# A chain of four graph layers on one core: 64 of 196 source record gathers made in the first convolution, and ScalarE's second-product copy placed later in the prefill

## The chip, the cores and the metric

The program runs on one core of one Trainium2 chip. The time is the device time of one execution in microseconds (us), 3544.22 as the median of three runs (3536.5 to 3548.16). Engines: PE is TensorE, DVE VectorE, ACT ScalarE, POOL GpSimd; SP only issues plain transfers. POOL issues the gathers (indirect DMAs). A cut-off "q" (SPq) is an engine's sequencer.

## The reference, cut to what matters

50,000 nodes with 128 features, 25,000 edges sorted by destination. Four graph layers, each added to its input and layer-normalised. The change touches the work of the first one:

```python
def _gcn_conv(x, W, b, src, dst, dinv, n_nodes):
    h = x @ W
    norm = dinv[src] * dinv[dst]
    msgs = h[src] * norm[:, None]
    out = segment_sum(msgs, dst, num_segments=n_nodes)   # src, dst with a self loop for every node
    return out + b

h = relu(_gcn_conv(x, W1, b1, src, dst, dinv, N))
x = layernorm(x + _gcn_conv(h, W2, b2, src, dst, dinv, N))
x = layernorm(x + mean of 8 relations)       # 8 weights and a root
x = layernorm(x + attention over 8 relations)
x = layernorm(x + relu(sum over 16 relations))
```

## The kernel before, in words

Edges are padded to 25,088 = 49 steps of 4 tiles of 128 (`NB` = 49, `BT` = 4, `KT` = 196 tiles). Nodes are worked in 98 chunks of 4 x 128 rows (`NCH` = 98). A node without an incoming edge needs no gather: its two convolution products are dense. That is the prefill. Nodes with edges get their rows in the edge stages.

Stages run one after the other; each is a block in which every engine has its own program, ordered by semaphores, and between two stages all engines meet and POOL clears the semaphores.

**Prefill** (`prefill_stage`). Per chunk: SP loads 256 KB of x; PE turns it (L594), ACT copies it out of PSUM (`xT`, L646), PE multiplies by W1 (L634), ACT applies the relu (`hT`, L677), PE multiplies by W2 (L602), ACT copies that second product out of PSUM (`g1`, L653), DVE adds x and b2 and takes the statistics, ACT makes the standard deviation (`sd1`, L668), DVE the scale and shift, and ACT the normalised rows (`x1`, four instructions, L660). SP stores `g1` and `x1`, 256 KB each (L547). All is software-pipelined: in turn c ScalarE works on chunk c (`xT`, `hT`), c-1 (`g1`), c-2 (`sd1`) and c-3 (`x1`), and `g1` and `x1` have two buffers each, so a buffer is written only when its store of two chunks ago has landed. In the first 49 chunks DVE and PE also count each node's edges (one-hot rows, L692, L694; L610); after chunk 48 DVE makes from the counts a table with a record per node: the row that holds its result, and `dinv`. SP stores that table (`t_info`).

POOL meanwhile gathers: 196 times 128 rows of x by destination (L576, kept for all stages), and, once `t_info` has landed, 196 times 128 records of 8 bytes by source (`m_info`, L580). The stage ends when all of these have landed and all stores too.

**First convolution** (`edge_stage` with `CONV1`, 49 steps). POOL gathers 4 tiles of source rows a step (L1101) into one of two buffers; it may start on step s when ACT has read step s-2 (`scaled_ready`). ACT scales the rows by `norm_col` (L1139), and the nodes' own rows (L1144); PE sums both and turns them (L1263, L1264); DVE scans along equal destinations (L1329); PE, ACT, PE make the two products (L1249, L1165, L1276); ACT writes `c_new` (L1195) and SP stores it. The same engines work through 49 dense chunks of the next layer in the same turns (`DenseLayers`: L860, L867, L876, L885, L902). `norm_col` (all 196 tiles) and `row_int` are made from the records by two DVE instructions at the stage's start (L1295, L1296). The second convolution uses `row_int` as its gather index.

In one turn of the first convolution ScalarE's order is: `dense_sd`, `scaled`, `own`, `dense_x1T`, `hT`, `dense_x` (L885), `c_new`.

Of the kernel before, what the change touches and what calls it, by code (L numbers as in the profile page):

```python
# [16 lines left out]
BT = 4  # L17
# [3 lines left out]
KT = EP // TE  # L21
# [6 lines left out]
NA = TA // BT  # L28
FAR = 65536
PAD_DST, PAD_SRC, PAD_TYPE = 60000, 0, -1  # L30
EPS = 1e-5
SLOPE = 0.2
LOW = -1.0e30
# [7 lines left out]
def runs(b, first=0, last=NB - 1):  # L41

    return not static(b) or first <= b <= last
# [429 lines left out]
def prefill_stage(nc, io, m):  # L473


    with ExitStack() as ctx:
# [91 lines left out]
        @block.gpsimd  # L568
        def _(pool):
            pool.memset(lower[:, :], 1.0).then_inc(lower_ready, 1)  # L570
            hold(pool, lower_ready, 1)
            pool.affine_select(out=lower[:, :], in_=lower[:, :], compare_op=ALU.is_ge, fill=0.0, base=0,
                               pattern=[[1, P]], channel_multiplier=-1).then_inc(lower_ready, 1)

            for k in range(KT):
                pool.indirect_dma_start(m.xd[:, k * D:(k + 1) * D], None, io["x"],  # L576
                                        bass.IndirectOffsetOnAxis(ap=m.dst_int[:, k:k + 1], axis=0)).then_inc(gathered, 16)
            hold(pool, info_stored, 16)
            for k in range(KT):
                pool.indirect_dma_start(m.info[:, k, :], None, m.info_table,  # L580
                                        bass.IndirectOffsetOnAxis(ap=m.src_int[:, k:k + 1], axis=0)).then_inc(gathered, 16)
            hold(pool, gathered, 2 * KT * 16)

        @block.tensor
        def _(pe):
# [51 lines left out]
        @block.scalar  # L637
        def _(act):
            def body(c, slot, first_half):
                q, o = slot % 2, 1 - slot % 2  # L640
                s = c
                if runs(s, 0, END):
                    act.wait_ge(x_turned, s + 1)
                    if runs(s, 2, END):
                        act.wait_ge(xw1_done, s - 1)
                    act.activation(xT[:, q, :], T[q][:, :], ACT.Copy).then_inc(xT_copied, 1)  # L646
                s = c - 1
                if runs(s, 0, END):
                    act.wait_ge(hw2_done, s + 1)
                    if runs(s, 2, END):  # L650
                        act.wait_ge(g1_stored[o], of_slot(s - 2, o, 16))
                        act.wait_ge(z1_ready, s - 1)
                    act.activation(flat(g1[:, o]), U[o][:, :], ACT.Copy).then_inc(g1_ready, 1)  # L653
                s = c - 3
                if runs(s, 0, END):
                    act.wait_ge(scale1_ready, s + 1)
                    if runs(s, 2, END):
                        act.wait_ge(x1_stored[o], of_slot(s - 2, o, X1_STORES[o]))
                    for j in range(BT):
                        last = act.activation(x1[:, o, j, :], z1[:, o, j, :], ACT.Identity,  # L660
                                              bias=shift1[:, o, j:j + 1], scale=scale1[:, o, j:j + 1])
                    last.then_inc(x1_ready, 1)
                s = c - 2
                if runs(s, 0, END):
                    act.wait_ge(mv1_ready, s + 1)
                    if runs(s, 1, END):
                        act.wait_ge(scale1_ready, s)
                    act.activation(sd1[:, :], mv1[:, :, 1], ACT.Sqrt, bias=m.eps[:, 0:1]).then_inc(sd1_ready, 1)  # L668
                if static(c) and c == HALF:
                    act.wait_ge(degree_ready, 1)  # L670
                    act.activation(root_of[:, :], degree[:, :], ACT.Sqrt, bias=m.ones[:, 0:1]).then_inc(rooted, 1)
                s = c
                if runs(s, 0, END):
                    act.wait_ge(xw1_done, s + 1)
                    if runs(s, 2, END):
                        act.wait_ge(hw2_done, s - 1)
                    act.activation(hT[:, q, :], H[q][:, :], ACT.Relu, bias=m.b1[:, 0:1]).then_inc(hT_ready, 1)  # L677
            chunks(act, body)

        @block.vector  # L680
        def _(v):
# [121 lines left out]
            def body(c, slot, first_half):  # L803
# [7 lines left out]
            chunks(v, body)  # L811


def rows_of(table, chunk):
# [170 lines left out]
def edge_stage(nc, io, m, kind, source, out, weights=None, n_rel=0):  # L985
# [5 lines left out]
    with ExitStack() as ctx:  # L991
# [18 lines left out]
        if kind == CONV2:  # L1010
# [19 lines left out]
            sem(n) for n in ("summed", "stats_ready", "scale_ready", "biased_ready", "squared", "norm_ready",  # L1030
                             "own_ready"))
        var_ready, sd_ready, shift_ready = sem("var_ready"), sem("sd_ready"), sem("shift_ready")
        T, H, B, S = m.psum[0:2], m.psum[2:4], m.psum[4:6], m.psum[6:8]
        LAST = NB - 1
        index = {CONV1: m.src_int, ATTEND: m.slot_int}.get(kind, m.row_int)
# [55 lines left out]

        @block.gpsimd
        def _(pool):
            for b in range(-2, NB + 3):
                s = b + 2
                if runs(s, 0, LAST):
                    if runs(s, 2):
                        hold(pool, turned if factor is None else scaled_ready, s - 1)
                    for j in range(BT):
                        k = s * BT + j  # L1100
                        pool.indirect_dma_start(rows[:, s % 2, j, :], None, source,  # L1101
                                                bass.IndirectOffsetOnAxis(ap=index[:, k:k + 1], axis=0))\
                            .then_inc(gathered[s % 2], 16)
                    if recorded is not None:
                        for j in range(2):
                            k = first_recorded + s * 2 + j
                            pool.indirect_dma_start(m.order8, bass.IndirectOffsetOnAxis(ap=m.order_int[:, k:k + 1], axis=0),  # L1107
                                                    m.row_int[:, k:k + 1], None, bounds_check=P * TA - 1, oob_is_err=False)\
                                .then_inc(recorded, 16)
                s = b - lag  # L1110
                if kind == SUM and runs(s, 0, LAST):
                    hold(pool, new_ready, s + 1)
                    for j in range(BT):
                        k = s * BT + j
                        pool.indirect_dma_start(out, bass.IndirectOffsetOnAxis(ap=m.last_int[:, k:k + 1], axis=0),  # L1115
                                                new[:, s % 2, j, :], None, bounds_check=NP - 1, oob_is_err=False)\
                            .then_inc(kept[s % 2], 16)
            if recorded is not None:
                hold(pool, recorded, KT // 2 * 16)
            if kind == SUM:  # L1120
                for q in range(2):
                    hold(pool, kept[q], of_slot(LAST - (LAST - q) % 2, q, KEPT))

        @block.scalar
        def _(act):
            if kind == CONV1:
                act.wait_ge(norm_ready, 3)

            def body(b, q):
                o = 1 - q  # L1130
# [161 lines left out]
        @block.vector  # L1292
        def _(v):
            if kind == CONV1:
                v.tensor_tensor(m.norm_col[:, :], m.info[:, :, 1], m.dinv_col[:, :], ALU.mult).then_inc(norm_ready, 1)  # L1295
                v.tensor_copy(m.row_int[:, :], m.info[:, :, 0]).then_inc(norm_ready, 1)  # L1296
                v.tensor_tensor(squares[:, :], m.dinv_col[:, :], m.dinv_col[:, :], ALU.mult).then_inc(squared, 1)
                v.wait_ge(squared, 1)
                v.tensor_tensor(self_col[:, :], squares[:, :], m.ends_col[:, :], ALU.mult).then_inc(norm_ready, 1)

            def relate(s, q, relations):

# [54 lines left out]
            def normalise(s, q):  # L1357

                if kind == CONV1 or not runs(s, 0, LAST):
# [4 lines left out]
                v.scalar_tensor_tensor(out=shift[:, q, :], in0=norm[1][:, :, 0], scalar=-1.0, in1=scale[:, q, :],  # L1364
                                       op0=ALU.mult, op1=ALU.mult).then_inc(shift_ready, 1)

            def add_b2(s, q):
# [25 lines left out]
            def body(b, q):  # L1393
                o = 1 - q
                if conv:
                    if kind == CONV1:
                        add_b2(b - 4, q)
                    scan(b - 1, o)
                    if kind == CONV1:
# [345 lines left out]
def build(nc, io):  # L1745
# [13 lines left out]
    with ExitStack() as ctx:  # L1759
# [14 lines left out]
            sb(n, [P, KT], I32) for n in ("dst_int", "hi_int", "lo_int", "src_int", "last_int", "row_int"))  # L1774
        m.order_int, m.slot_int, m.tile_type = sb("order_int", [P, KT], I32), sb("slot_int", [P, KT], I32), sb("tile_type", [1, TA], I32)
        m.info = sb("info", [P, KT, 2])
        m.xd = sb("xd", [P, KT * D])
        constants_stage(nc, m)
        with nc.sbuf_tensor("m_halo", [QR, 258], I32) as m.halo, nc.sbuf_tensor("m_rows", [QR, 4, 256], I32) as m.rows:
# [39 lines left out]
```

## Time and profile before

| what | value |
|---|---|
| median of three runs | 3544.22 us (3536.5 to 3548.16) |
| the profiled execution | 3547.79 us, its span 3546.1 us |
| busy share of the span | PE 68%, DVE 68%, POOL 63%, ACT 48%, PE weight loads 43% |
| mean granted TensorE clock | 0.835 of full speed |
| prefill | 61.7 to 609 us of the span |
| first convolution | 610 to 965 us |
| source record gathers | 196, 1001 ns each, 338 to 600 us |

A share of the whole span says little here, since every stage has another limit. The trace is therefore read stage by stage: which engine idles, and for whom.

### The profile page before, as it was taken

What the parts mean: (1) busy time and instruction counts of PE and PEld (TensorE: products, weight loads), DVE (VectorE), ACT (ScalarE), POOL (GpSimd) and SP (SyncE); (2) the same over time, 40 slices, a digit from 0 to 9 for tenths busy, and PEclk for the clock granted to TensorE, in tenths of its full rate; (3) what the DMA queues carried; (4) which work ended last, traced back from release to release, by engine and by line L of the source; (5) the groups of instructions that cost most, each with busy time, mean ns of one, the idle gap of its engine ahead of it and who ended that gap; (6) DMA issues with size and microseconds to landing.
All of it is one profiled execution on the core that took longest, in us unless ns stands there. A gap on an engine that the chain in (4) does not pass through costs nothing. (4 is left out here: it accounts for less than half of the span.)

```text
span 3546.1 us, 55088 instructions
## 1 busy us (share of the span) xinstructions
PE 2412.7 (68%) x9989; PEld 1522.5 (43%) x9990; DVE 2423.7 (68%) x7395; ACT 1716.3 (48%) x4719; POOL 2219.3 (63%) x2178
## 2 busy tenths in 40 slices
PE   2775761777655665999976765453233599999997
PEld 1443440666555654344433335443222244444443
DVE  7998661788778886899961112223566588888886
ACT  1774772888745554455444445554577311111111
POOL 2777776555377774777747766552666366666664
PEclk9997885999878887999988995555555699999998
DMA  2664552555445443333327776554577411111111
GB/s 64 215 215 145 173 178 62 157 172 173 149 126 152 147 149 94 82 91 91 93 82 244 255 238 168 167 172 138 150 206 211 124 40 45 48 49 50 51 52 34
DMA packets 294009, 465.22 MB, mean 131 GB/s; under 512 B 65978, under 2 KB 120793, under 8 KB 293930
## 3 DMA queue, kind: packets, MB, share of 16 engines
q1 hardware_dynamic: 224682, 351.70, 30.9%
q0 software_dynamic: 69248, 112.70, 13.1%
q14 instruction: 59, 0.48, 0.0%
q8 instruction: 20, 0.33, 0.0%
HBM read 247.81 MB, written 220.22 MB: 132 GB/s over the span
## 5 line engine op out<-in xcount | busy, mean ns | idle before, releaser
L1221 PE MATMUL bank<-sum_masked,sum_w 128*128 128x512 f32 x1568 | 691.2, 594 | 1.4 <-DVE sum_masked L1311 1.4
L1311 DVE SCALAR_TENSOR_TENSOR sum_masked<-sum_typ,sum_col 128x512 f32<-128x512 bf16 x784 | 488.6, 683 | 19.4 <-ACT sum_col L1151 17.3
L1221 PEld LDWEIGHTS bank<-sum_masked,sum_w 128*128 128x128 f32 x1568 | 291.4, 191 | 332.3 <-issue 268.9
L1221 PE MATMUL bank<-mean_masked,mean_w 128*128 128x512 f32 x784 | 376.7, 610 | 18.9 <-DVE mean_masked L1311 18.9
L1101 POOL DMA_INDIRECT sum_rows<-t_x,m_row_int x196 | 224.3, 1144 | 239.2 <-PE bank L1267 168.6
L1151 ACT ACTIVATE sum_col<-bank 128x512 f32<-128x512 f32 x49 | 29.3, 597 | 578.9 <-PE bank L1267 565.4
L1101 POOL DMA_INDIRECT mean_rows<-t_x,m_row_int x196 | 233.7, 1192 | 101.0 <-issue 57.3
L1514 POOL DMA_INDIRECT at_us<-t_u,m_slot_int x196 | 185.2, 945 | 148.8 <-PE bank L1633 79.7
L1101 POOL DMA_INDIRECT c_rows<-x_dram,m_src_int x196 | 185.3, 945 | 147.0 <-ACT c_scaled L1139 90.7
L1101 POOL DMA_INDIRECT att_rows<-t_h,m_slot_int x196 | 185.2, 945 | 141.0 <-POOLq L94 54.8
L1115 POOL DMA_INDIRECT out_dram<-sum_new,m_last_int x196 | 218.5, 1115 | 87.5 <-issue 67.2
L1311 DVE SCALAR_TENSOR_TENSOR mean_masked<-mean_typ,mean_col 128x512 f32<-128x512 bf16 x392 | 252.6, 686 | 17.1 <-ACT mean_col L1151 17.1
L1504 POOL DMA_INDIRECT at_xs<-t_x,at_order x204 | 192.9, 945 | 100.1 <-issue 63.8
L1101 POOL DMA_INDIRECT c_rows<-t_g,m_row_int x196 | 188.7, 963 | 99.2 <-issue 55.8
L576 POOL DMA_INDIRECT m_xd<-x_dram,m_dst_int x196 | 207.7, 1060 | 64.5 <-issue 64.5
L580 POOL DMA_INDIRECT m_info<-t_info,m_src_int x196 | 196.2, 1001 | 69.3 <-issue 66.0
L1107 POOL DMA_INDIRECT order<-m_row_int,m_order_int x196 | 198.5, 1013 | 59.7 <-issue 59.7
L602 PE MATMUL bank<-m_w,pf_hT 128*128 128x128 f32 x784 | 126.0, 309 | 142.6 <-ACT pf_hT L677 142.6
L1221 PEld LDWEIGHTS bank<-mean_masked,mean_w 128*128 128x128 f32 x784 | 130.3, 190 | 196.3 <-DVE mean_masked L1311 151.0
L1525 DVE COPY at_made<-bank 128x512 f32<-128x512 f32 x51 | 35.3, 691 | 251.3 <-PE bank L1601 251.3
L1652 DVE TENSOR_TENSOR_SCAN at_dst<-at_nxt,at_dst,bank 128x512 f32<-128x512 bf16 x48 | 61.4, 1280 | 203.9 <-DMA at_nxt<-p_next 202.6
L1601 PE MATMUL bank<-at_both,at_xsT 128*128 x408 | 154.3, 475 | 64.1 <-issue 61.5
(322 smaller groups left out, 6045.7 us busy)
## 6 DMA issues: line engine op xcount, KB each, us to landing
pf_xc<-x_dram SPq DMA_DIRECT2D x98, 256.0 KB, 3.0
t_g<-pf_g SPq DMA_DIRECT2D x98, 256.0 KB
t_x<-pf_x SPq DMA_DIRECT2D x98, 256.0 KB
c_dense_x<-t_x SPq DMA_DIRECT2D x98, 256.0 KB, 3.4
t_x<-c_dense_x SPq DMA_DIRECT2D x98, 256.0 KB, 3.4
t_h<-at_made SPq DMA_DIRECT2D x51, 256.0 KB, 3.1
t_u<-at_made SPq DMA_DIRECT2D x51, 256.0 KB, 3.6
c_same<-p_same SPq DMA_DIRECT2D x98, 128.0 KB, 3.4
```

Of the source, the lines that this page charges most:

```text
L576: pool.indirect_dma_start(m.xd[:, k * D:(k + 1) * D], None, io["x"], bass.IndirectOffsetOnAxis(ap=m.dst_int[:, k:k + 1], axis=0)).then_inc ...
L580: pool.indirect_dma_start(m.info[:, k, :], None, m.info_table, bass.IndirectOffsetOnAxis(ap=m.src_int[:, k:k + 1], axis=0)).then_inc(gathe ...
L602: last = pe.matmul(U[o][:, j * D:(j + 1) * D], hT[:, o, j * D:(j + 1) * D], m.w2[:, :], start=True, stop=True)
L1101: pool.indirect_dma_start(rows[:, s % 2, j, :], None, source, bass.IndirectOffsetOnAxis(ap=index[:, k:k + 1], axis=0))\
L1107: pool.indirect_dma_start(m.order8, bass.IndirectOffsetOnAxis(ap=m.order_int[:, k:k + 1], axis=0), m.row_int[:, k:k + 1], None, bounds_che ...
L1115: pool.indirect_dma_start(out, bass.IndirectOffsetOnAxis(ap=m.last_int[:, k:k + 1], axis=0), new[:, s % 2, j, :], None, bounds_check=NP - ...
L1221: pe.matmul(H[q][:, :], w[:, r, :], masked[:, r % MASKS, :], start=(r == 0), stop=(r == n_rel - 1))\
L1311: v.scalar_tensor_tensor(out=masked[:, r % MASKS, :], in0=typ[:, q, :], scalar=float(r), in1=col[:, q, :], op0=ALU.is_equal, op1=ALU.mult) ...
L1504: pool.indirect_dma_start(xs[:, s % 2, j, :], None, m.tables["X2"], bass.IndirectOffsetOnAxis(ap=order[:, k:k + 1], axis=0))\
L1514: pool.indirect_dma_start(us[:, s % 2, j, :], None, m.tables["U"], bass.IndirectOffsetOnAxis(ap=m.slot_int[:, k:k + 1], axis=0))\
L1601: last = pe.matmul(M[q][j // 2][:, (j % 2) * 2 * D:(j % 2 + 1) * 2 * D], xsT[:, q, j * TE:(j + 1) * TE], both[:, bass.ds(r * (2 * D), 2 * D)],
L1652: v.tensor_tensor_scan(dst[:, q, ::-1], nxt[:, q, ::-1], TD[q][:, ::-1], start, ALU.mult, ALU.add)\
```

## The change

64 of the 196 source record gathers (`INFO_LATE`) are no longer made in the prefill. In the first convolution POOL issues four of them behind the rows of every second step, 0 to 30. `norm_col` is made per step on DVE (49 instructions on 128x4 in place of one on 128x196), each waiting for the records by count, and ScalarE's `scaled` waits for it. `row_int` is made at the start of the second convolution, and POOL waits for it there. In the prefill ScalarE's copy `g1` stands behind `x1` instead of ahead of it.

```diff
@@ prefill, POOL
-            for k in range(KT):
-                pool.indirect_dma_start(m.info[:, k, :], None, m.info_table, ...).then_inc(gathered, 16)
-            hold(pool, gathered, 2 * KT * 16)
+            for k in range(KT - INFO_LATE):
+                gather_info(pool, m, k)
+            hold(pool, gathered, KT * 16)
+            hold(pool, m.info_gathered, (KT - INFO_LATE) * 16)
@@ prefill, ScalarE, in body(c, slot, first_half)
                     act.activation(xT[:, q, :], T[q][:, :], ACT.Copy).then_inc(xT_copied, 1)
-                s = c - 1
-                    ...
-                    act.activation(flat(g1[:, o]), U[o][:, :], ACT.Copy).then_inc(g1_ready, 1)
                 s = c - 3
                     ...
                     last.then_inc(x1_ready, 1)
+                s = c - 1
+                    ...
+                    act.activation(flat(g1[:, o]), U[o][:, :], ACT.Copy).then_inc(g1_ready, 1)
                 s = c - 2
@@ edge_stage, POOL
+            if kind == CONV2:
+                hold(pool, rows_known, 1)
@@
+                    if kind == CONV1 and s % 2 == 0 and s // 2 < INFO_LATE // BT:
+                        for j in range(BT):
+                            gather_info(pool, m, KT - INFO_LATE + s // 2 * BT + j)
@@ edge_stage, ScalarE
+                    if kind == CONV1:
+                        act.wait_ge(norm_ready, s + 1)
@@ edge_stage, DVE
-                v.tensor_tensor(m.norm_col[:, :], m.info[:, :, 1], m.dinv_col[:, :], ALU.mult).then_inc(norm_ready, 1)
-                v.tensor_copy(m.row_int[:, :], m.info[:, :, 0]).then_inc(norm_ready, 1)
+            if kind == CONV2:
+                v.tensor_copy(m.row_int[:, :], m.info[:, :, 0]).then_inc(rows_known, 1)
@@
+            def norms(s):
+                v.wait_ge(m.info_gathered, (s + 1) * BT * 16)
+                v.tensor_tensor(at(m.norm_col, s), m.info[:, bass.ds(s * BT, BT), 1], at(m.dinv_col, s), ALU.mult)\
+                    .then_inc(norm_ready, 1)
```

POOL's order from the prefill into the first convolution, before (`m_xd` are the destination rows, `m_info` the source records, `c_rows` the source rows; the branches and the ISA row are the meeting of the engines and the clearing of semaphores):

```order
L576 DMA m_xd<-x_dram,m_dst_int 128x128 x196
L580 DMA m_info<-t_info,m_src_int 128x2 x196
L476 UNCONDITIONAL_BRANCH
L95 UNCONDITIONAL_BRANCH
L98 ISA x36
L94 UNCONDITIONAL_BRANCH
L1092 UNCONDITIONAL_BRANCH
L1101 DMA c_rows<-x_dram,m_src_int 128x128 x196
```

And with the change, POOL at the same place, down to step 6:

```order
L577 DMA m_xd<-x_dram,m_dst_int 128x128 x196
L817 DMA m_info<-t_info,m_src_int 128x2 x132
L477 UNCONDITIONAL_BRANCH
L96 UNCONDITIONAL_BRANCH
L99 ISA x36
L95 UNCONDITIONAL_BRANCH
L1100 UNCONDITIONAL_BRANCH
L1111 DMA c_rows<-x_dram,m_src_int 128x128 x4
L817 DMA m_info<-t_info,m_src_int 128x2 x4
L1111 DMA c_rows<-x_dram,m_src_int 128x128 x8
L817 DMA m_info<-t_info,m_src_int 128x2 x4
L1111 DMA c_rows<-x_dram,m_src_int 128x128 x8
```

64 gathers have left the row ahead of the meeting, and stand in fours among the rows of the first 32 steps: 12 gathers where there were 8 in every two steps. Behind them the remaining rows follow as before.

ScalarE's order in a turn of the prefill, before (`pf_g` is the copy `g1`, `pf_x` the rows `x1`):

```order
L646 ACTIVATE pf_xT<-bank 128x512
L653 ACTIVATE pf_g<-bank 128x512
L660 ACTIVATE pf_x<-pf_z,pf_shift,pf_scale 128x128 x4
L668 ACTIVATE pf_sd<-pf_mv,m_eps 128x4
L677 ACTIVATE pf_hT<-bank,m_b 128x512
```

And ScalarE's order in the same turn with the change:

```order
L647 ACTIVATE pf_xT<-bank 128x512
L654 ACTIVATE pf_x<-pf_z,pf_shift,pf_scale 128x128 x4
L663 ACTIVATE pf_g<-bank 128x512
L669 ACTIVATE pf_sd<-pf_mv,m_eps 128x4
L678 ACTIVATE pf_hT<-bank,m_b 128x512
```

The copy has moved past four instructions; each of the two keeps the waits that it had (the copy for PE's second product, the rows for their scale and for the landing of a store).

## Rows read from the trace of the kernel before

**Rows 1.** Busy time by stretch: PE, PEld, DVE, ACT, POOL (count), clock, DMA share, GB/s.

```profile
62.00:295.00 233.00, 164.95 (x889) 111.14 (x890) 216.77 (x971) 168.14 (x385) 176.13 (x172) 0.96 0.66 211
332.00:536.00 204.00, 142.55 (x630) 94.18 (x630) 132.17 (x540) 151.23 (x358) 149.54 (x148) 0.82 0.57 177
640.00:945.00 305.00, 228.46 (x1700) 192.52 (x1699) 249.00 (x941) 275.32 (x849) 162.55 (x173) 1.00 0.55 171
```

**Rows 2.** Timeline of POOL: start, duration, instruction, idle time before it and releaser.

```profile
599.23 0.94 POOL L580 DMA_INDIRECT m_info<-t_info,m_src_int  x1 [0.30 <-issue]
610.15 0.99 POOL L1101 DMA_INDIRECT c_rows<-x_dram,m_src_int  x1 [9.97 <-POOLq L94]
```

**Rows 3.** The dense work's end: SP's last store, and busy time by stretch.

```profile
555.13 0.33 SPq L547 DMA_DIRECT2D t_x<-pf_x  x1
...
556.00:557.00 1.00, 0.00 (x0) 0.00 (x0) 0.00 (x0) 0.00 (x0) 0.69 (x2) 0.50 0.72 257
```

**Rows 4.** Timeline of the first convolution's end: DVE's last instruction, POOL's next.

```profile
963.35 1.14 DVE L1382 SCALAR_TENSOR_TENSOR m_xd<-c_new,m_dinv_col,c_biased 128x128 f32<-128x128 f32 x4
968.92 0.94 POOL L1101 DMA_INDIRECT c_rows<-t_g,m_row_int  x1 [36.45 <-POOLq L94]
```

**Rows 5.** ScalarE's groups from 332 to 536 us: busy, mean ns, idle before.

```profile
L653 ACT ACTIVATE pf_g<-bank 128x512 f32<-128x512 f32 x45 | 26.9, 597 | 50.7 <-PE bank L602 42.6 <-DVE pf_z L797 8.1
```

**Rows 6.** Timelines of ACT, DVE and SP, one turn of the prefill's second half.

```profile
442.09 1.65 ACT L660 ACTIVATE pf_x<-pf_z,pf_shift,pf_scale 128x128 f32<-128x128 f32 x4
443.65 0.28 ACT L668 ACTIVATE pf_sd<-pf_mv,m_eps 128x4 f32<-128x4 f32 x1
...
443.96 0.18 DVE L779 RECIPROCAL pf_scale<-pf_sd 128x4 f32<-128x4 f32 x1 [1.03 <-ACT pf_sd L668]
...
444.98 0.69 DVE L797 TENSOR_TENSOR pf_z<-pf_g,pf_xb 128x512 f32<-128x512 f32 x1
...
447.00 0.33 SPq L547 DMA_DIRECT2D t_x<-pf_x  x1
```

**Rows 7.** How long a store takes to land: SP and ACT timelines, DMA issues (KB each, median us).

```profile
233.20 0.33 SPq L547 DMA_DIRECT2D t_x<-pf_x  x1
...
236.75 1.64 ACT L660 ACTIVATE pf_x<-pf_z,pf_shift,pf_scale 128x128 f32<-128x128 f32 x4 [0.56 <-DMA t_x<-pf_x]
...
t_x<-c_dense_x SPq DMA_DIRECT2D x98, 256.0 KB, 3.4
...
t_x<-m_xd SPq DMA_DIRECT2D x49, 256.0 KB, 4.3
```

**Rows 8.** Timeline of PE, a turn at the lower clock.

```profile
444.55 2.08 PE L602 MATMUL bank<-m_w,pf_hT 128*128 128x128 f32 x8 [0.55 <-ACT pf_hT L677]
446.42 1.91 PE L634 MATMUL bank<-pf_xT,m_w 128*128 128x512 f32 x2
```

**Rows 9.** Timelines of POOL, PE and ACT, a step of the first convolution.

```profile
749.97 0.94 POOL L1101 DMA_INDIRECT c_rows<-x_dram,m_src_int  x1 [2.14 <-ACT c_scaled L1139]
...
751.01 0.46 PE L1263 MATMUL bank<-m_ident,c_scaled 128*128 128x128 f32 x2 [1.73 <-ACT c_own L1144]
...
754.15 1.14 ACT L1195 ACTIVATE c_new<-bank,m_dinv_col 128x128 f32<-128x128 f32 x4 [0.69 <-PE bank L1276]
```

**Rows 10.** Timeline of ACT: `scaled` of steps 0, 31 and 32.

```profile
616.78 1.27 ACT L1139 ACTIVATE c_scaled<-c_rows,m_norm_col 128x128 f32<-128x128 f32 x4 [61.67 <-DMA c_rows<-x_dram,m_src_int]
...
823.65 1.28 ACT L1139 ACTIVATE c_scaled<-c_rows,m_norm_col 128x128 f32<-128x128 f32 x4
830.48 1.28 ACT L1139 ACTIVATE c_scaled<-c_rows,m_norm_col 128x128 f32<-128x128 f32 x4
```

**Rows 11.** POOL's groups: 337.9 to 560 us, 560 to 601, 640 to 931.

```profile
L580 POOL DMA_INDIRECT m_info<-t_info,m_src_int x164 | 166.0, 1012 | 59.6 <-issue 56.2 <-DMA t_info<-pf_info_rows 3.4
...
L580 POOL DMA_INDIRECT m_info<-t_info,m_src_int x33 | 31.2, 944 | 10.1 <-issue 10.1
...
L1101 POOL DMA_INDIRECT c_rows<-x_dram,m_src_int x172 | 162.5, 945 | 129.9 <-ACT c_scaled L1139 90.3 <-issue 39.7
```

More of the change, by code:

```diff
@@ L30 @@
 PAD_DST, PAD_SRC, PAD_TYPE = 60000, 0, -1
+INFO_LATE = 64
 EPS = 1e-5
@@ L646, in body @@
                     act.activation(xT[:, q, :], T[q][:, :], ACT.Copy).then_inc(xT_copied, 1)
-                s = c - 1
[L648 to L652, printed above, removed]
-                    act.activation(flat(g1[:, o]), U[o][:, :], ACT.Copy).then_inc(g1_ready, 1)
                 s = c - 3
@@ L662, in body @@
                     last.then_inc(x1_ready, 1)
+                s = c - 1
+                if runs(s, 0, END):
+                    act.wait_ge(hw2_done, s + 1)
+                    if runs(s, 2, END):
+                        act.wait_ge(g1_stored[o], of_slot(s - 2, o, 16))
+                        act.wait_ge(z1_ready, s - 1)
+                    act.activation(flat(g1[:, o]), U[o][:, :], ACT.Copy).then_inc(g1_ready, 1)
                 s = c - 2
@@ L811, in _, with gather_info @@
             chunks(v, body)
+def gather_info(pool, m, k):
+    pool.indirect_dma_start(m.info[:, k, :], None, m.info_table,
+                            bass.IndirectOffsetOnAxis(ap=m.src_int[:, k:k + 1], axis=0)).then_inc(m.info_gathered, 16)
 def rows_of(table, chunk):
@@ L1032, in edge_stage @@
         var_ready, sd_ready, shift_ready = sem("var_ready"), sem("sd_ready"), sem("shift_ready")
+        self_ready, rows_known = sem("self_ready"), sem("rows_known")
         T, H, B, S = m.psum[0:2], m.psum[2:4], m.psum[4:6], m.psum[6:8]
@@ L1126, in _ @@
             if kind == CONV1:
-                act.wait_ge(norm_ready, 3)
+                act.wait_ge(self_ready, 1)
             def body(b, q):
@@ L1294, in _ @@
             if kind == CONV1:
-                v.tensor_tensor(m.norm_col[:, :], m.info[:, :, 1], m.dinv_col[:, :], ALU.mult).then_inc(norm_ready, 1)
-                v.tensor_copy(m.row_int[:, :], m.info[:, :, 0]).then_inc(norm_ready, 1)
                 v.tensor_tensor(squares[:, :], m.dinv_col[:, :], m.dinv_col[:, :], ALU.mult).then_inc(squared, 1)
                 v.wait_ge(squared, 1)
-                v.tensor_tensor(self_col[:, :], squares[:, :], m.ends_col[:, :], ALU.mult).then_inc(norm_ready, 1)
+                v.tensor_tensor(self_col[:, :], squares[:, :], m.ends_col[:, :], ALU.mult).then_inc(self_ready, 1)
+            if kind == CONV2:
+                v.tensor_copy(m.row_int[:, :], m.info[:, :, 0]).then_inc(rows_known, 1)
             def relate(s, q, relations):
@@ L1365, in normalise @@
                                        op0=ALU.mult, op1=ALU.mult).then_inc(shift_ready, 1)
+            def norms(s):
+                if not runs(s, 0, LAST):
+                    return
+                v.wait_ge(m.info_gathered, (s + 1) * BT * 16)
+                v.tensor_tensor(at(m.norm_col, s), m.info[:, bass.ds(s * BT, BT), 1], at(m.dinv_col, s), ALU.mult)\
+                    .then_inc(norm_ready, 1)
             def add_b2(s, q):
@@ L1396, in body @@
                     if kind == CONV1:
+                        norms(b + 2)
                         add_b2(b - 4, q)
@@ L1776, in build @@
         m.info = sb("info", [P, KT, 2])
+        m.info_gathered = nc.alloc_semaphore("info_gathered")
         m.xd = sb("xd", [P, KT * D])
```

2 lines of the change are left out of this document (removed).

## The prediction

> **What bounds the kernel now.** Stages follow one another, so I read the trace by stretches first: busy time of each engine in each [rows 1]. The reader is to see three regimes. In the prefill's first half VectorE is busy 216.77 of 233 us and bounds it. In the second half no engine is: ScalarE, the busiest, has 151.23 of 204 us, so a ring of waits bounds it. In the first convolution ScalarE has 275.32 of 305 us and bounds it.
>
> Next the ends of the two stages, in the timelines. POOL's last record gather of the prefill starts at 599.23 and the first convolution's first gather at 610.15 [rows 2]. The dense work was done long before: SP's last store goes out at 555.13, and its transfer is the one stretch with busy DMA, 556 to 557 [rows 3]. So from 557 to 602 the kernel waits for POOL alone, and POOL's row of gathers is what ends the prefill.
>
> Then the idle time inside the two rings, from the groups and timelines. In the prefill ScalarE stands 50.7 us, in 45 turns, ahead of the copy of the second product, 42.6 of it for PE [rows 5]. In the first convolution POOL waits 2.14 us a step for ScalarE to free a buffer [rows 9], 90.3 us from 640 to 931 [rows 11]. These are the two covers on which the change draws.
>
> **The change part by part.** The sum is made against the profiled execution, 3547.79 us (span 3546.1), which is 3.6 us above the median of the runs shown, 3544.22.
>
> *1. 64 gathers leave the prefill.* Beside the dense work a record gather takes 1.012 us and 0.34 between two: (166.0 + 56.2)/164 = 1.355 [rows 11]. POOL begins them at 338; 132 end at 338 + 132 x 1.355 = 517. Then the dense work is last, at 557. From the end of everything to POOL's next gather there are two rows to go by: the first convolution's end, where VectorE stops at 964.5 and POOL starts at 968.92, 4.4 us [rows 4], and the prefill's own, where the last gather leaves POOL at 600.2 and the next starts 10 us later [rows 2], some 8 of them after it can have landed. I take the first, since here too POOL will have stopped earlier: 557.2 + 4.4 = 562 in place of 610: 48 us less. By the other it is 44.
>
> *2. The copy behind the normalised rows.* A turn takes 204/45 = 4.53 us [rows 1, 5]. The wait ahead of the copy goes, since four instructions (442.09 to 443.65, 1.56 us [rows 6]) now stand in it. What is late next? The rows come 1 us or so earlier in the turn, and they wait for the store of two turns ago. That ring, from [rows 6]: rows 1.56, copy 0.60 [rows 5], deviation to VectorE's start 0.31, to the end of the sum `pf_z` 1.71 (443.96 to 445.67), to SP's store 1.33 (447.00), landing 3.4 (the median of stores of this size in the first convolution, under about the same 170 GB/s [rows 1, 7]), together 8.91 for two turns: 4.46 a turn. Before, the copy was not in this ring: 8.31, 4.16 a turn, hidden. The other limit is PE at its lower clock (1.2 GHz): 1.87 from the second product to the next first one and 1.91 for that one [rows 8], and the relu's copy and the handovers, some 0.75: 4.53. The granted clock is 0.82 in this half [rows 1], so 1.2 GHz in about 36% of the time. 0.64 x 4.46 + 0.36 x 4.53 = 4.49: 0.04 x 49 turns = 2 us less. In the first half VectorE's 233/49 = 4.75 a turn stays above 4.46: nothing. Ends: the whole wait gone would give 50.7/45 x 49 = 55 us, but POOL's own end, 517 + 10 = 527, cuts that to 35; a landing of 3.55, as in the first half [rows 7], gives 4.53, nothing; one of 4.3, the slowest median in the trace [rows 7], gives 4.9, and 18 us more. I take 2, by the row nearest in load.
>
> *3. The 64 gathers in the first convolution.* POOL's four gathers a step take 0.945 each and 0.30 between two, 1.245 [rows 11]; a record gather takes the same when nothing runs beside it, 0.944 and 0.31 [rows 11]. In two steps POOL has now 12: 14.94 us. Two steps of ScalarE take 13.67 (830.48 - 823.65 = 6.83 [rows 10]). So the cover does not do: POOL becomes the bound of the first 32 steps. 16 x 14.94 = 239, and 1.65 until ScalarE starts on the landed rows (610.15 + 4 x 1.245 to 616.78): the scaling of step 31 starts 240.7 after the first gather. Before it was 823.65 - 610.15 = 213.5. Afterwards ScalarE goes on at 6.83 a step as before: 27 us more. Ends: 0, if ScalarE's waits took all of it; 16 x 12 x 1.355 + 1.65 - 213.5 = 48, if gathers are as slow as in the prefill. I take 27, since the 172 rows of this very stage all but agree on 945 ns.
>
> The Trainium skill, on the page SBUF — State Buffer (section Who interferes with whom), holds that a VectorE instruction that reads two SBUF operands contends with a GpSimd instruction that reads SBUF. The first convolution's VectorE has such instructions [rows 4], and yet its gathers take 945 ns against 944 with VectorE idle [rows 11]: this trace does not show it. By the rule part 3 would stand at its upper end, 48, and the sum at about 0.
>
> *4. The small things.* The norm per step: 49 VectorE instructions, which the trace does not show in this shape; VectorE has 56 us free in 305 [rows 1], and works a step ahead of ScalarE. ScalarE's third wait ahead of `scaled`, and the wait of the second convolution's first gather for `row_int`: VectorE's first instruction stands ahead of POOL's start in both stages. Together 1 us, between 0 and 5 (0.1 a step).
>
> *Sum:* -48 - 2 + 27 + 1 = -22. 3547.8 - 22 = 3525.8 by the profiled execution, and 3522 by the median.
>
> **The rivals.**
>
> *The copy pays more.* If stores land faster than 3.4, or PE stays at 2.4 GHz, the turn falls to 4.2: 0.33 x 49 = 16 instead of 2: 3508; 35 would give 3489. For it: the 50.7 us of waiting are real, and no row of this half shows a wait for a store ahead of `pf_x` worth naming. Against: the ring above.
>
> *The store's landing becomes the bound in earnest.* At 4.3 us the prefill gets 18 longer: 3542, no change that can be told. For it: in the first half ScalarE waits 0.56 us for a landing even now [rows 7]. Against: the second half moves 177 GB/s, not 211 [rows 1].
>
> *ScalarE stays the bound of the first convolution*, POOL's extra work lying wholly in its waits: part 3 is 0, 3495. Against: 14.94 is more than 13.67, and no order of issue changes that.
>
> *PE's clock falls in the first convolution: the slower end.* There PE is busy 228 of 305 us, with a gap of 1.73 us a step [rows 9], and the clock is 1.00 throughout [rows 1]; in the prefill's second half it is busy 143 of 204 and the clock is 0.82. With POOL as the bound, ScalarE waits 1.3 us more for rows in every second step, and so does PE. From its first matmul at 751.01 to the copy `c_new` at 754.15 stand 3.1 us [rows 9], and ScalarE waits for their end (0.69 [rows 9]); at 1.2 GHz they take up to 2.9 more, and a step 9.7. In one of two steps: 16 x 16.5 + 1.65 - 213.5 = 52 instead of 27: 3547. In both: 16 x 19.4 gives 98, 3593, slower. It decides from about 49 us on, or 16.4 us for two steps. Against: a slower PE fills its own gaps, so the state would end itself.
>
> The Trainium skill has this as a rule, on the page TensorE: Matmul & The Clock Gate (section HAM oscillation): a loop in which PE waits for a transfer every time round can begin every round at the low clock. The prefill's 0.82 bears it out; the first convolution's 1.00, with its gap each step, does not.
>
> **How the numbers follow.** My forecast, POOL as the bound of 32 steps and the copy worth little, has 0.50; the copy paying more 0.17; the landing as bound 0.13; the first convolution unhurt 0.04; the clock lost in one of two steps 0.10, in both 0.06. Less than 0.3% (10.6 us: below 3533.6 or above 3554.9) is about what a measurement of this kernel can't tell from no change. Faster: 0.46 of the forecast's 0.50, 0.17, 0.04 and 0.03 of the landing's: 0.70. Same: 0.04 + 0.10 + 0.08 = 0.22. Slower: 0.02 + 0.06 = 0.08. The range: down to 3494, which leaves out the last of the copy's gain, and up to 3549, which takes in the landing at 4.3 and the clock lost in one step of two; the forecast's own is 3508 to 3535.
>
> **What the profile after would show.** POOL's last record gather of the prefill ends near 517, and the first convolution's first gather starts near 560 (527 if the copy pays in full, 580 if the landing binds). In the prefill ScalarE's wait ahead of the copy is gone and one ahead of `pf_x` for `t_x` stands in its place; a turn of the second half takes 4.4 to 4.5. In the first convolution POOL issues without waits until step 31, two steps take 14.9 to 15.2, ScalarE waits for `c_rows` once in two steps, and the granted clock stays above 0.9; then 6.83 a step. The stage is 27 longer, from the second convolution on all lengths are as before. The forecast is wrong if the prefill's end moves by less than 40 or more than 65 us, or if the 32 steps take more than 250.

## The result, and the profile after

The changed kernel takes 3521.35 us (median of 5 runs, 3516.07 to 3523.27) against 3541.32 us before (5 runs, 3536.5 to 3548.16): a ratio of 0.9939, with a 95% interval from 0.9923 to 0.9955. It is 20 us faster, and the whole interval lies beyond the 0.3% below which a change can't be told from none. The profiled execution takes 3523.27 us (span 3521.5).

The two ends of stages, in the timelines of SP, POOL and VectorE after the change (start, duration, instruction, idle time before it and its releaser; SP's line stands for three stores in a row, of which the last leaves at 546.79 + 6.24 - 0.33 = 552.7):

```profile
546.79 6.24 SPq L548 DMA_DIRECT2D t_x<-pf_x  x3
...
514.32 1.39 POOL L817 DMA_INDIRECT m_info<-t_info,m_src_int  x1 [0.31 <-issue]
558.39 0.95 POOL L1111 DMA_INDIRECT c_rows<-x_dram,m_src_int  x1 [42.68 <-POOLq L95]
...
950.14 0.26 DVE L1314 CAST m_row_int<-m_info 128x196 int32<-128x196 f32 x1 [3.91 <-PEq L95]
950.76 0.94 POOL L1111 DMA_INDIRECT c_rows<-t_g,m_row_int  x1 [36.56 <-DVE m_row_int L1314]
```

Read them against [rows 2 to 4]. The record gathers of the prefill now end at 514.32 + 1.39 = 515.7, and POOL then stands 42.7 us until the dense work is done: the two have changed places. The first convolution's first gather moves from 610.15 to 558.39, 51.8 us earlier. The second convolution's first gather moves from 968.92 to 950.76, only 18.2 earlier. So the stage between them has grown from 358.8 to 392.4: 33.6 us of the gain are given back there. From 950.76 to the span's end stand 2570.7 us against 2577.2 before; in the eight kernels below it is 2568 to 2575, so the profiled execution of before was some 5 us long in stages that the change doesn't touch.

Busy time by stretch after the change, columns as in [rows 1]:

```profile
62.00:295.00 233.00, 159.32 (x887) 108.74 (x888) 216.70 (x970) 163.42 (x385) 175.60 (x173) 0.98 0.66 211
332.00:536.00 204.00, 133.79 (x630) 91.58 (x630) 132.66 (x544) 154.84 (x361) 133.85 (x133) 0.87 0.57 180
566.00:700.00 134.00, 91.82 (x615) 79.98 (x616) 86.14 (x333) 97.60 (x298) 101.70 (x107) 0.89 0.45 135
700.00:811.00 111.00, 79.94 (x552) 68.76 (x551) 83.42 (x312) 88.03 (x271) 84.49 (x88) 0.94 0.51 156
811.00:930.00 119.00, 89.22 (x665) 75.16 (x664) 98.95 (x378) 107.21 (x330) 58.94 (x61) 1.00 0.53 166
```

VectorE still bounds the first half. The first convolution falls into two parts. From 700 to 811 us ScalarE is busy 88.03 of 111 us, in place of nine tenths, and the clock is below 1.00; once the records are in, it is busy 107.21 of 119 and the clock is 1.00 again.

ScalarE's groups from 332 to 520 us (count, busy us, mean ns, idle time before and who ended it), the two that changed places:

```profile
L654 ACT ACTIVATE pf_x<-pf_z,pf_shift,pf_scale 128x128 f32<-128x128 f32 x166 | 68.4, 482 | 37.3 <-DMA t_x<-pf_x 37.0
...
L663 ACT ACTIVATE pf_g<-bank 128x512 f32<-128x512 f32 x41 | 23.6, 576 | 0.9 <-PE bank L603 0.8
```

The wait for PE ahead of the copy [rows 5] is gone. In its place ScalarE waits 37.0 us for the store of `t_x` ahead of the normalised rows. One round of that wait, in the timelines of ACT, DVE and SP:

```profile
440.56 0.48 ACT L654 ACTIVATE pf_x<-pf_z,pf_shift,pf_scale 128x128 f32<-128x128 f32 x1
442.75 0.72 DVE L798 TENSOR_TENSOR pf_z<-pf_g,pf_xb 128x512 f32<-128x512 f32 x1
443.71 0.35 SPq L556 DMA_DIRECT2D pf_xc<-x_dram  x1
...
444.80 0.33 SPq L548 DMA_DIRECT2D t_x<-pf_x  x1
...
448.17 1.65 ACT L654 ACTIVATE pf_x<-pf_z,pf_shift,pf_scale 128x128 f32<-128x128 f32 x4 [0.42 <-DMA t_x<-pf_x]
```

The last of a turn's four row instructions ends at 441.04. SP sends their store only at 444.80, behind a load that has waited for VectorE's sum (`pf_z`) and behind the second product's store, and the rows of two turns later start when that store has landed, 3.4 us after it left.

The first convolution from inside: POOL's groups from 558 to 806 us, then ScalarE's timeline from step 28 (772.53) to step 32 (803.34 is step 31).

```profile
L1111 POOL DMA_INDIRECT c_rows<-x_dram,m_src_int x132 | 127.0, 962 | 82.6 <-POOLq L95 42.7 <-issue 39.6 <-ACT c_scaled L1154 0.3
L817 POOL DMA_INDIRECT m_info<-t_info,m_src_int x64 | 61.7, 964 | 19.5 <-issue 19.5
```

```profile
769.74 1.14 ACT L1210 ACTIVATE c_new<-bank,m_dinv_col 128x128 f32<-128x128 f32 x4 [0.69 <-PE bank L1291]
772.53 1.27 ACT L1154 ACTIVATE c_scaled<-c_rows,m_norm_col 128x128 f32<-128x128 f32 x4 [1.55 <-DMA c_rows<-x_dram,m_src_int]
779.87 1.14 ACT L1210 ACTIVATE c_new<-bank,m_dinv_col 128x128 f32<-128x128 f32 x4 [2.31 <-PE bank L1291]
780.99 1.28 ACT L1154 ACTIVATE c_scaled<-c_rows,m_norm_col 128x128 f32<-128x128 f32 x4
...
787.89 1.28 ACT L1154 ACTIVATE c_scaled<-c_rows,m_norm_col 128x128 f32<-128x128 f32 x4
...
794.73 1.28 ACT L1154 ACTIVATE c_scaled<-c_rows,m_norm_col 128x128 f32<-128x128 f32 x4
...
803.34 1.28 ACT L1154 ACTIVATE c_scaled<-c_rows,m_norm_col 128x128 f32<-128x128 f32 x4 [1.64 <-DMA c_rows<-x_dram,m_src_int]
810.68 1.14 ACT L1210 ACTIVATE c_new<-bank,m_dinv_col 128x128 f32<-128x128 f32 x4 [2.31 <-PE bank L1291]
811.80 1.28 ACT L1154 ACTIVATE c_scaled<-c_rows,m_norm_col 128x128 f32<-128x128 f32 x4
```

POOL no longer waits for ScalarE (0.3 us, where [rows 11] has 90.3 from 640 to 931): it issues without a pause. From 680 us on ScalarE waits for rows once in four steps, at 772.53 and again at 803.34, 30.8 us apart. PE then stands longer too, and its next matmuls run at 1.2 GHz. Its timeline in the step that ScalarE began at 741.80, after 1.28 us of waiting, and in the next:

```profile
744.39 0.46 PE L1278 MATMUL bank<-m_ident,c_scaled 128*128 128x128 f32 x2 [3.14 <-ACT c_own L1159]
...
744.94 0.64 PE L1278 MATMUL bank<-m_ident,c_scaled 128*128 128x128 f32 x2
...
753.38 0.39 PE L1278 MATMUL bank<-m_ident,c_scaled 128*128 128x128 f32 x2
```

Two matmuls take 0.64 us after an idle time of 3.14, and 0.39 one step later. In such a step the wait ahead of `c_new` is 2.31 instead of 0.69. It did not follow every time: at 668.04 PE had stood 3.34 us, and the wait ahead of `c_new` was 0.68.

### The profile page after: what moved, and what is told of

Read it like the earlier page. It is cut to its first block and busy times, and to the rows that moved or that the text cites. A ratio compares the mean times of both kernels' runs of the same rounds, so it can differ in the third digit from the quotient of the medians.

```text
span 3521.5 us, 55329 instructions
## 1 busy us (share of the span) xinstructions
PE 2412.6 (69%) x9989; PEld 1531.5 (43%) x9990; DVE 2431.6 (69%) x7443; ACT 1714.9 (49%) x4719; POOL 2218.4 (63%) x2178
## 5 line engine op out<-in xcount | busy, mean ns | idle before, releaser
L654 ACT ACTIVATE pf_x<-pf_z,pf_shift,pf_scale 128x128 f32<-128x128 f32 x392 | 161.4, 482 | 113.0 <-DMA t_x<-pf_x 99.7
```

## The experiments

Two theories stood against each other. Mine: the prefill was ended by POOL's record gathers alone; with 64 of them gone the dense work ends it; the copy is worth next to nothing, because the wait for a store takes the place of the wait for PE; and the 33.6 us given back are the time that POOL needs to issue 64 gathers more than ScalarE leaves it. The rivals: that the copy carries the gain, and that records cost by themselves in the first convolution, by contention or the clock.

The places that tell them apart, in us, from the profiled executions (the first gather of each convolution), with the time of all runs beside them (“gathers only” to “64 records, two a step” ran beside a before of 3545.49, the last four beside one of 3548.06, the change beside 3541.32):

| kernel | conv. 1 | conv. 2 | between | median | ratio to before (95%) |
|---|---|---|---|---|---|
| before | 610.15 | 968.92 | 358.8 | | 1 |
| the change | 558.39 | 950.76 | 392.4 | 3521.35 | 0.9939 (0.9923–0.9955) |
| gathers only | 556.74 | 950.25 | 393.5 | 3526.07 | 0.9940 (0.9927–0.9953) |
| copy only | 610.93 | 970.21 | 359.3 | 3547.12 | 1.0004 (0.9994–1.0014) |
| 44 records, one a step | 559.98 | 922.97 | 363.0 | 3499.75 | 0.9864 (0.9849–0.9880) |
| 64 records, two a step | 558.27 | 947.48 | 389.2 | 3522.96 | 0.9931 (0.9918–0.9945) |
| rows stored first | 525.10 | 918.88 | 393.8 | 3490.27 | 0.9840 (0.9827–0.9853) |
| rows stored first, copy back | 559.69 | 950.68 | 391.0 | 3517.72 | 0.9915 (0.9901–0.9928) |
| rows first, 44 records | 552.04 | 916.58 | 364.5 | 3489.89 | 0.9837 (0.9822–0.9852) |
| rows first, 64 spread | 526.19 | 896.88 | 370.7 | 3468.29 | 0.9780 (0.9767–0.9794) |

**Gathers only.** The change, with the copy back in its old place:

```diff
+                s = c - 1            # the copy of the second product
+                ...
                 s = c - 3            # the normalised rows
                 ...
-                s = c - 1
-                ...
```

> The 64 gathers moved as in the change, the copy of the second product left where it was before, ahead of the normalised rows. Theory (the gathers carry the gain, the copy is worth 2 us): the first convolution's first gather at 561 to 563 us against 558.4 after the change, the idle time ahead of the copy in the second half back at 45 to 55 us, the one ahead of the rows for the store of t_x gone; total 3523 to 3527. Rival (the copy carries most of the gain): total back at 3535 to 3542, with the first convolution's first gather at 575 or later.

Measured: 0.9940, the ratio of the whole change. The first gather comes at 556.74, 1.7 us earlier than with the copy moved, where I had expected it 3 to 5 later. The two groups of ScalarE from 332 to 520 us have changed back:

```profile
L661 ACT ACTIVATE pf_x<-pf_z,pf_shift,pf_scale 128x128 f32<-128x128 f32 x168 | 68.7, 482 | 1.9 <-DMA t_x<-pf_x 1.8
...
L654 ACT ACTIVATE pf_g<-bank 128x512 f32<-128x512 f32 x42 | 25.1, 597 | 43.3 <-PE bank L603 34.2 <-DVE pf_z L798 9.1
```

So 43.3 us of waiting at one place or 37.3 at the other, and the same time within the intervals of the two ratios (some 5 us each way): the copy's place carries no part of the gain that can be measured.

**Copy only.** The kernel before, with the copy moved as in the change and nothing else.

> The copy alone moved behind the normalised rows, all 196 record gathers in the prefill as before. Theory: POOL's last gather still starts near 599 us and ends the prefill, the first convolution's first gather stays at 610 (within 2), and the total is that of before within 3 us, although SP's last store leaves 2 to 5 us earlier. Rival (the copy carries the gain): 3521 to 3530.

Measured: 1.0004, no change. POOL's timeline shows the end of the prefill where it was:

```profile
599.80 0.94 POOL L580 DMA_INDIRECT m_info<-t_info,m_src_int  x1 [0.30 <-issue]
610.93 0.98 POOL L1101 DMA_INDIRECT c_rows<-x_dram,m_src_int  x1 [10.19 <-POOLq L94]
```

I had expected SP's last store to leave 2 to 5 us earlier. It left at 550.37 + 6.25 - 0.33 = 556.3 (again the last of three), against 555.13 [rows 3]: the copy's move alone makes the dense work no shorter either.

**44 records, one a step.**

```diff
-INFO_LATE = 64
+INFO_LATE = 44
-                    if kind == CONV1 and s % 2 == 0 and s // 2 < INFO_LATE // BT:
-                        for j in range(BT):
-                            gather_info(pool, m, KT - INFO_LATE + s // 2 * BT + j)
+                    if kind == CONV1 and s < INFO_LATE // 1:
+                        for j in range(1):
+                            gather_info(pool, m, KT - INFO_LATE + s * 1 + j)
```

> 44 record gathers in place of 64 in the first convolution, one in each of the first 44 steps in place of four in every second of 32. Theory (their price there is POOL's time for issuing them): a step of POOL is 5 x 1.245 = 6.2 us, below the 6.83 of ScalarE, so the stage costs 0 to 6 us more than before instead of 33.6; POOL's prefill ends at 338 + 152 x 1.355 = 544, before the dense work; total 3490 to 3500. Rival (each record gather costs there by itself, by contention or by the clock): 44/64 of 33.6 = 23 us, total 3508 to 3514.

Measured: 3499.75, and the stage takes 4.2 us more than before instead of 33.6. By the rival it would have been 23. POOL's groups from 566 to 811 us:

```profile
L1111 POOL DMA_INDIRECT c_rows<-x_dram,m_src_int x148 | 143.8, 972 | 56.2 <-issue 38.1 <-ACT c_scaled L1154 18.1
L817 POOL DMA_INDIRECT m_info<-t_info,m_src_int x36 | 34.0, 944 | 11.0 <-issue 11.0
```

With five gathers a step POOL waits for ScalarE again, 18.1 us: the records lie in the cover and cost next to nothing. The clock is 1.00 from 600 to 811 us. Of the 4.2 us, 2.7 are gone by step 7, whose `scaled` starts 52.04 us after the first gather (612.02 - 559.98) in place of 49.37 (659.52 - 610.15): in these first steps ScalarE still waits for rows. So the records' price is that of POOL's issuing, and only beyond what ScalarE's step leaves free.

**64 records, two a step.** The same number as in the change, spread evenly over the same 32 steps: `s < INFO_LATE // 2`, and `range(2)` in place of `range(BT)`.

> The same 64 record gathers, two in each of the first 32 steps in place of four in every second one. Theory (POOL is the bound of these steps): six gathers a step, 7.5 us, give the same 32 steps within 4 us, except for what the dips of PE's granted clock every fourth step cost (1.6 us each, some 8 to 12 us in all), since PE's gaps are now even: clock 0.98 to 1.00 in 600 to 811 us, total 3512 to 3521. Rival (ScalarE's long wait in every second step is what costs, not POOL's sum of issues): the stage costs less than 10 us more than before, total below 3500.

Measured: 3522.96. The stage takes 30.4 us more than before, 3.2 less than after the change; the total, expected at 3512 to 3521, is level with that of the change. The rival (the uneven steps cost, not the sum) falls. But my reason for a gain falls too: the clock is not restored. Busy time by stretch:

```profile
566.00:700.00 134.00, 93.06 (x627) 80.70 (x628) 88.32 (x336) 98.75 (x299) 101.72 (x106) 0.92 0.46 137
700.00:811.00 111.00, 78.75 (x548) 66.77 (x548) 85.18 (x321) 91.39 (x280) 84.46 (x88) 0.95 0.51 153
```

0.92 and 0.95, against 0.89 and 0.94 after the change and 0.98 to 1.00 expected. The 3.2 us have a simpler source, worked out and not isolated: the last step's four rows now stand ahead of its two records, behind 62 records instead of 64, and 2 x 1.265 is 2.5.

**Rows stored first.** This asks what the second half of the prefill waits for after the change. On SP, the store of the normalised rows goes ahead of the turn's load and of the second product's store:

```diff
+                store(c - 4, q, x1_ready, "X1", x1, x1_stored)
                 s = c + LOAD_AHEAD
                 if runs(s, 0, END):
                     if runs(s, 4, END):
                         hold(sp, z1_ready, s - 3)
                     sp.dma_start(xc[:, (slot + LOAD_AHEAD) % 4], rows_of(io["x"], s))\
                         .then_inc(loaded[(slot + LOAD_AHEAD) % 4], 16)
                 store(c - 2, q, g1_ready, "G1", g1, g1_stored)
-                store(c - 4, q, x1_ready, "X1", x1, x1_stored)
```

> The change, and in the prefill SP sends the store of the normalised rows ahead of the turn's load and of the second product's store. Theory (after the copy's move the turn's ring goes through SP's order: the rows' store stands behind a load that waits for VectorE's sum, and the rows of two turns later wait for its landing): ScalarE's wait for t_x ahead of pf_x in 332 to 520 us, 37 us after the change, falls below 10; a turn takes 4.1 to 4.3 instead of 4.5; the first convolution's first gather at 541 to 549 instead of 558.4; total 3504 to 3512. Rival (the landing itself is slow, or PE's matmuls at the lower clock hold the turn): gather at 556 or later, total within 3 of 3521.

Measured: 3490.27, 31 us below the change (35 by the two ratios), and more than the theory gave: the first gather comes at 525.10, where 541 to 549 was expected. ScalarE's groups, columns and stretch as above:

```profile
L654 ACT ACTIVATE pf_x<-pf_z,pf_shift,pf_scale 128x128 f32<-128x128 f32 x200 | 81.9, 485 | 1.6 <-DVE pf_shift L782 0.9 <-DMA t_x<-pf_x 0.7
...
L663 ACT ACTIVATE pf_g<-bank 128x512 f32<-128x512 f32 x48 | 27.9, 582 | 0.3 <-DMA t_g<-pf_g 0.2
```

Both waits are gone. Timeline of ACT and SP, one turn:

```profile
440.74 1.64 ACT L654 ACTIVATE pf_x<-pf_z,pf_shift,pf_scale 128x128 f32<-128x128 f32 x4
...
442.92 0.33 SPq L548 DMA_DIRECT2D t_x<-pf_x  x1
...
444.26 1.64 ACT L654 ACTIVATE pf_x<-pf_z,pf_shift,pf_scale 128x128 f32<-128x128 f32 x4
```

The rows end at 442.38 and their store goes out at 442.92, 0.5 us later; after the change it went out up to 3.8 us after the rows' end (441.04 to 444.80 above). This turn takes 3.5 us. Over the 50 turns of the half the mean by VectorE's `pf_scale` is 3.6, (506.73 - 327.26)/50, in place of 4.4, (550.62 - 329.25)/50. Busy time by stretch, where I look for what made it more than expected:

```profile
332.00:505.00 173.00, 118.15 (x661) 81.24 (x659) 141.49 (x577) 161.50 (x385) 129.15 (x124) 0.98 0.70 222
```

I had counted with PE's matmuls and the handovers as before. Now ScalarE, busy 161.5 of 173 us, is the bound, and the granted clock is 0.98, against 0.87 with the wait (332 to 536 us after the change). No run separates the two: the faster turn may be owed to the clock, or the clock to the faster turn. The Trainium skill has a rule (TensorE: Matmul & The Clock Gate, section HAM oscillation) that a loop in which PE waits for a transfer in every round can begin each round at the low clock. The two figures go the way of that rule but do not test it, since PE waits here for ScalarE's `pf_hT` and not for a transfer, and does so in both kernels (70.5 us of idle time from 332 to 505 us after the change, 51.5 here). For the same reason the prefill's 0.82, which the prediction says bears the rule out, is no test of it [rows 8]. The dense work is now done before POOL. Timelines of SP and POOL:

```profile
505.41 3.73 SPq L548 DMA_DIRECT2D t_x<-pf_x  x2
...
517.42 0.95 POOL L817 DMA_INDIRECT m_info<-t_info,m_src_int  x1 [0.30 <-issue]
525.10 0.96 POOL L1111 DMA_INDIRECT c_rows<-x_dram,m_src_int  x1 [6.73 <-POOLq L95]
```

SP's last store leaves at 505.41 + 3.73 - 0.33 = 508.8, POOL's last gather ends at 518.4: the 132 gathers that stay in the prefill end it again.

**Rows stored first, copy back.** The same order on SP, and the copy ahead of the rows again.

> The same order on SP, with the copy of the second product back in its place ahead of the normalised rows. Theory (with the copy ahead, ScalarE waits for PE and not for a store, so the order on SP is worth nothing there; the copy's move pays only together with it): the wait for PE ahead of the copy stays at 40 to 55 us, first gather at 555 to 559, total 3519 to 3527. Rival (SP's order alone makes the turn): as the kernel with the rows' store first and the copy moved.

Measured: 3517.72, 1.3 us below what was expected, with the first gather at 559.69, 0.7 above; ScalarE's group of the copy from 332 to 520 us:

```profile
L654 ACT ACTIVATE pf_g<-bank 128x512 f32<-128x512 f32 x41 | 24.5, 597 | 49.2 <-PE bank L603 42.2 <-DVE pf_z L798 7.0
```

With "gathers only", the change itself and "rows stored first" this makes a square: copy ahead or behind, load or rows first on SP. In the profiled executions three of its four corners (556.74, 558.39, 559.69) are the same within 3 us, the fourth is 525.10: each ring alone is as long as the other, and only with both cut does the turn fall. The times are not quite as even. This corner's ratio is 0.9915, against 0.9940 and 0.9939 for the other two: some 9 us less, with intervals that just touch. Its profiled execution, 3523.69, is the longest of its five (3514.17 to 3523.69), so the profile does not show where the others are shorter, and whether SP's order alone is worth nothing or these 9 us stays open. With the copy moved it gives 35.

**Rows first, 44 records.** The edits of "rows stored first" and "44 records, one a step" together.

> The rows' store first on SP, and 44 record gathers in the first convolution, one a step. Theory: the dense work ends before 545, but POOL has 152 gathers in the prefill, ending at 544, and its next gather follows 10 us after the last as before the change: first gather at 552 to 556; the stage 363 long as with one a step; total 3489 to 3496. Rival (the end follows the dense work): first gather at 541 to 549, total 3481 to 3488.

Measured: first gather at 552.04, total 3489.89, both as the theory had them. POOL ends its 152 gathers at 543.4 and starts again 8.6 us later, although SP's last store of the prefill had left at 505.44 + 3.73 - 0.33 = 508.8: here POOL alone ends the prefill.

**Rows first, 64 spread.** The same order on SP; the 64 records two and one in turn over 43 steps:

```diff
+                    if kind == CONV1:
+                        for k in range((3 * s + 1) // 2, min((3 * s + 4) // 2, INFO_LATE)):
+                            gather_info(pool, m, KT - INFO_LATE + k)
```

> The rows' store first on SP, and 64 record gathers in the first convolution, two and one in turn over 43 steps. Theory: POOL has 5.5 gathers a step, 6.85 us, against ScalarE's 6.83, so the stage costs 3 to 12 us more than before instead of 33.6, and POOL's prefill ends at 517, ahead of the dense work: first gather at 541 to 549, total 3478 to 3490. Rival (records cost by themselves, or two rings of one length hold each other up): the stage 20 or more longer than before, total 3495 or more.

Measured: 3468.29, a ratio of 0.9780 (0.9767 to 0.9794), the fastest kernel here. The stage takes 11.9 us more than before, within what was expected; the total is below it, because the first convolution begins at 526 and not after 541, as with "rows stored first". Busy time by stretch, and POOL's groups from 558 to 806 us:

```profile
566.00:700.00 134.00, 98.31 (x706) 83.15 (x706) 107.57 (x415) 116.56 (x359) 101.75 (x106) 0.97 0.54 165
700.00:811.00 111.00, 82.80 (x620) 70.02 (x619) 93.78 (x356) 100.05 (x308) 84.47 (x88) 1.00 0.57 173
...
L1111 POOL DMA_INDIRECT c_rows<-x_dram,m_src_int x142 | 137.7, 970 | 43.3 <-issue 43.3
L817 POOL DMA_INDIRECT m_info<-t_info,m_src_int x54 | 51.4, 952 | 16.5 <-issue 16.5
```

POOL issues without a pause here too, the same 88 gathers in 700 to 811 us as after the change. But at 5.5 a step they serve 16 steps and not 14.7, and ScalarE, busy 100.05 of 111 us, no longer waits for rows in that stretch: the two engines run at about the same rate. Of the 11.9 us, 6.6 are gone by step 7 (582.20 - 526.19 = 56.0 in place of 49.4), where ScalarE still waits for rows.

## Why the prediction was right, step by step

**Part 1, the gathers leave the prefill: right.** POOL was to end at 517 and ended at 515.7; the first convolution was to begin at 560 (562 less the copy's 2) and began at 558.4. "Copy only" (no change) and "gathers only" (all of the gain) show that this part alone carries it.

**Part 2, the copy: the mechanism right, the 2 us not.** I had said that the wait for PE would go and one for `t_x` take its place, in a ring through SP's order, 4.46 us a turn. The wait did move, 37.0 us of it, the landing took the 3.4 us that I had used, a turn takes 4.4, and "rows stored first" shows that SP's order makes the ring. But the other ring is as long: with the copy moved the first gather comes 0.8 and 1.7 us later (610.93 against 610.15, 558.39 against 556.74), and the medians show nothing within some 5. PE at the lower clock, 4.53 a turn in the prediction, did not hold the turn: with the store out of the ring it fell to 3.6, at a granted clock of 0.98. SP's last store does leave 2.4 us earlier after the change (552.7 against 555.13), as the sum had it, but it leaves earlier still with the copy in its old place (551.1) and not at all earlier with the copy alone (556.3). The few microseconds go with the gathers that have left; what they do to the dense work was not isolated.

**Part 3, the gathers in the first convolution: the mechanism right, 27 too small.** POOL is the bound of 32 steps, as forecast, and not of a step more. To step 31 it is 803.34 - 558.39 = 245.0 us in place of 240.7. A gather takes 963 ns here and not 945 (127.0 + 61.7 us for 196): 192 x 0.018 = 3.5 of these 4.3 us. Step 31 itself then takes 8.46 us instead of 6.83, since PE's matmuls run at 1.2 GHz after the wait for rows ahead of it (the granted clock is 0.79 from 803 to 811 us): 1.6 more. Together 27 + 4.3 + 1.6 = 33; the table has 33.6, the small things in it. This is the error of the forecast: 6 us of 27. Two signs that the prediction gave for this stage were missed: ScalarE waits for rows once in four steps and not in two, and two steps take 15.4 us (30.8/2) and not 14.9 to 15.2. A third only just held: the granted clock, which was to stay above 0.9, is 0.91 from 566 to 811 us, with 0.89 in the first part.

By its reading of the Trainium skill's rule on VectorE and GpSimd (SBUF — State Buffer, section Who interferes with whom) the prediction put this part at its upper end, 48. The runs lie far below that: 963 ns against 945, single gathers up to 1.44 us. What stretches them, no run here tells.

**Part 4, the small things: next to nothing.** The norm of a step takes VectorE 0.16 us, and no wait of ScalarE in the trace is for it; VectorE itself waits 3.0 us, in six steps, for records. The second convolution's first gather waits for `row_int`, but VectorE's cast ends 0.4 us before it, and the handover is about as long as before: 4.5 us from the end of VectorE's last instruction of the stage (945.08 + 1.14) to POOL's first gather at 950.76, against 4.4 [rows 4].

**The sum.** -51.8 + 33.6 = -18.2 us up to the second convolution, where -22 was forecast with errors of 2 and 6 of opposite sign. The median difference is 20 us. That the total came out within 1 us of the 3522 forecast is luck: the two errors partly cancel, and the median of before came out 3 us lower than the 3544.22 that the forecast started from.

**The rivals.** That the copy pays more: refuted by two kernels, although the 50.7 us of waiting were real; they were to be had only together with SP's order. That the landing becomes the bound in earnest: no, the turn is 4.4 us, and the landing shown above 3.4. That the first convolution is unhurt: refuted at 64 records, nearly true at 44 with one a step (4.2 us). That the clock falls there: it does, from 680 us on in every fourth step, but while POOL is the bound the slower PE costs nothing save in the last step.

## What to carry to other kernels

Work that an engine does for free is free only up to the time its neighbour's step leaves: add up the engine's issues per step before and after, and spread the added ones over so many steps that each stays below the bound (44 gathers at one a step cost 4.2 us, 64 spread over 43 steps 11.9, 64 in bursts over 32 steps 33.6, and 64 evenly over the same 32 steps 30.4: the sum per step counts, not the evenness). When a wait goes, look for the ring that is as long as the one it closed, above all through a queue that issues in order: here moving the copy was worth nothing, reordering the queue little (9 us by the ratios, none in the profile), and both 35. After each gain look again at what ends the stage last; here it was POOL, then the dense work, then POOL.

## What the runs showed that I had not expected

POOL spends the same 0.95 + 0.30 us on an indirect gather of 128 records of 8 bytes as on one of 128 rows of 512 bytes (964 and 962 ns above): between these two sizes the price is by the instruction, not by its bytes.

PE's granted clock rose with the gain when a wait went: 0.87 to 0.98 in the second half of the prefill, and a turn fell to 3.6 us where 4.1 to 4.3 was expected from the durations of before. How much of the difference is the clock's was not isolated.
